# Attention maxima turned by VectorE in 32x32 blocks and placed by eight transfers, instead of one TensorE transpose, one ScalarE copy and two transfers

## The chip, the cores and the metric

The kernel runs on one core of one Trainium2 chip. The metric is the device time of one execution in microseconds (us); three runs of the kernel before gave a median of 2221.6 us (2217.65 to 2241.77 us).

## The reference

One transformer block on `x` of 8 sequences, 1024 tokens each, 256 features, all float32. First attention with 16 heads of 16 features, then a mixture of 8 experts. What matters here is the attention, where keys and values are the same projection:

```python
q = x @ Wq
kv = x @ Wkv
q, kv = rotary(split(q)), rotary(split(kv))     # (8 * 16 heads, 1024, 16)
q = q * SCALE
att = jnp.einsum('bmd,bnd->bmn', q, kv)
attn = jax.nn.softmax(att, axis=-1)
out = jnp.einsum('bij,bjd->bid', attn, kv)
```

The softmax subtracts each row's maximum before the exponential.

## The kernel before, in words

The program has four parts, one after the other with small overlaps: projection (`project`), attention (`attend`), what finishes the attention and chooses tokens, and the experts. The change touches only `attend`.

**Pairs and groups.** Attention works on 64 pairs of heads (8 sequences, 8 pairs each). A pair takes 16 groups (`NG = 16`). In each group TensorE does, in `body` of `tensor`: two score products of the pair (`scores`, L681, into the ring `a_st` of three PSUM slots), two products for the row maxima of a later pair (`maxima`, L718, into the two slots of `a_sm`), and eight small products of probabilities and values (`values`, L705, into `a_pv`). ScalarE takes each score slot and writes its exponential to `a_prob` (`exp`, L844): 32 a pair. VectorE reduces each `a_sm` slot to negated maxima (`reduce`, L770): 16 a pair.

**The maxima of a pair are found one pair ahead.** In the second half of pair q's own groups and the first half of the next, maxima of the pair after are reduced: while pair q is scored, groups 0 to 7 finish the maxima of pair q+1 and groups 8 to 15 begin those of pair q+2. After group 7 VectorE combines the two halves (`a_nm`, L778). GpSimd cuts the result into a high and a low part (`split`, L809 and L811, into `a_nsplit`).

**From columns to rows.** The scores are taken transposed (keys on partitions, queries along the free dimension), so the maxima must be subtracted along the free dimension. The kernel does this inside the score product: the negated maxima stand as two extra rows (high and low part) of the query tile `a_q`, against rows of ones in `a_k`. The maxima come out of the reduction as columns, one per partition, and so must be turned into rows. Before the change this takes five steps, for pair q+1 during pair q: TensorE transposes `a_nsplit` into a slot of the score ring ahead of group 12 (`turn_maxima`, L689); ScalarE copies 32 rows of 128 from there to `a_mrow` (`copy_max_rows`, L858) and so frees the slot; SyncE issues two transfers `a_q<-a_mrow`, one per head (`max_rows`, L543); and TensorE's first score product of pair q+1 waits for them:

```python
if u == 0:
    pe.wait_ge(m_in, (q.n + 1) * 32)
```

**SyncE's queue.** SyncE (SP) issues all transfers of attention in one order per pair q (`body` of `sync`): nine loads for pair q+2 (`load`, L528 and L534), which wait until pair q-1 has all its scores; the reciprocals of pair q-2 (`put_rden`, L614); the raw output of pair q-1 (`store`, L642); the scaled output of pair q-3 (`put_on`, L624); `fetch_rden` of pair q-2 (L618); the maxima rows of pair q+1 (`max_rows`, L543); and two fetches of pair q-1 (`fetch`, L607 and L609). Each waits for what it needs, and everything behind it waits with it.

**GpSimd's order** per pair q is `split(q)`, `place(q+2)`, `scale(q-3)`:

```python
split(q)
if not q.first() and q.plus(2).exists():
    place(q.plus(2))
if q.follows(3):
    scale(pool, q.plus(-3))
```

`place` (L819) copies the values just loaded, the last of the nine loads, and waits for them to land. `scale` (L572) makes the result that `put_on` stores. So `put_on` for pair q-3 comes after the landing of the values of pair q+2, because GpSimd does the one behind the other.

**The start.** The rows of pair 0 are turned while TensorE makes maxima of pair 1. ScalarE itself issues their two transfers, while SyncE is still busy with the last stores of the projection.

## Time and profile before

| | us |
|---|---|
| median of three runs | 2221.6 |
| lowest and highest run | 2217.65, 2241.77 |
| the profiled execution's own time | 2217.65 |
| its span, first to last instruction | 2217.7 |
| attention, first score product to last exponential | 273.8 to 1586.2 |

The profile is of one execution, the 2217.65 us one; its span is its time. PE is TensorE's matrix products, PEld its weight loads, DVE is VectorE, ACT ScalarE, POOL GpSimd, SP SyncE; a q behind an engine's name means its instruction queue (SPq issues transfers). A row of the chronological view gives start, length, engine, line, operation, output and inputs, count, and in brackets how long the engine was idle before and what ended that.

### The profile page before, as it was taken

To read this page: it belongs to the slowest core of one execution; us is meant where nothing else is said; L and a number is where in the kernel's file an instruction comes from. 1 tells how busy PE (TensorE), PEld (TensorE's weight loads), DVE (VectorE), ACT (ScalarE), POOL (GpSimd) and SP (SyncE) were. 2 spreads that over 40 slices of the span, in tenths; PEclk is the share of its full clock that TensorE was granted. 3 is DMA by queue.
4 is the path that set the end of the run, shared out by engine and by line. 5 is a ranking of instruction groups with operands and counts; after the bars stand their busy time and mean duration, and the time that the engine had idled before them with its cause. 6 is when DMAs were issued, how large, how long until landed. Compare 5 with 4: busy or idle time off the path is not lost. (4 is left out here: it accounts for less than half of the span.)

```text
span 2217.7 us, 53241 instructions
## 1 busy us (share of the span) xinstructions
PE 2004.8 (90%) x16684; PEld 1046.9 (47%) x16684; DVE 1950.9 (88%) x3221; ACT 1503.4 (68%) x2842; POOL 648.3 (29%) x864
## 2 busy tenths in 40 slices
PE   6777699999999999999999999999988129999998
PEld 3344233333333333333333333333577128999997
DVE  7888889999999999999999999999489679888863
ACT  3444278888888888888888888888645014554443
POOL 7788300110111011011111101111277015565653
PEclk9999689999999999999999999999999559999999
DMA  2666644344344444434433443444476023443432
GB/s 88 219 222 214 183 116 77 71 82 86 71 78 83 77 73 83 83 72 80 83 76 74 82 85 70 80 83 90 143 257 205 30 79 82 101 93 85 103 66 29
DMA packets 152543, 224.62 MB, mean 101 GB/s; under 512 B 34855, under 2 KB 104970, under 8 KB 152458
## 3 DMA queue, kind: packets, MB, share of 16 engines
q1 hardware_dynamic: 131814, 197.89, 38.2%
q0 software_dynamic: 12288, 17.05, 4.5%
q10 hardware_dynamic: 8356, 8.67, 1.1%
q8 instruction: 39, 0.64, 0.1%
q14 instruction: 46, 0.38, 0.1%
HBM read 129.38 MB, written 93.06 MB: 100 GB/s over the span
## 5 line engine op out<-in xcount | busy, mean ns | idle before, releaser
L770 DVE TENSOR_REDUCE a_mx<-a_sm 128x2 f32<-128x1024 f32 x1024 | 1234.8, 1223 | 56.1 <-PE a_sm L718 42.8
L844 ACT ACTIVATE a_prob<-a_st 128x512 f32<-128x512 f32 x2048 | 1113.1, 597 | 170.7 <-PE a_st L681 139.7
L681 PE MATMUL a_st<-a_q,a_k 50*128 50x512 f32 x2048 | 752.9, 448 | 5.7 <-DMA a_q<-a_mrow 5.7
L718 PE MATMUL a_sm<-a_k,a_q 48*128 48x512 f32 x2048 | 748.0, 455 | 9.7 <-DVE a_mx L770 8.0
L705 PE MATMUL a_pv<-a_prob,a_v 128*32 128x256 f32 x8192 | 657.1, 393 | 23.1 <-ACT a_oraw L851 22.5
L681 PEld LDWEIGHTS a_st<-a_q,a_k 50*128 50x128 f32 x2048 | 312.3, 186 | 412.0 <-ACT a_prob L844 391.8
L819 POOL TENSOR_TENSOR a_v<-a_v_raw,a_zero 128x256 f32<-128x256 f32 x64 | 39.6, 620 | 1065.2 <-DMA a_v_raw<-values 1065.2
L705 PEld LDWEIGHTS a_pv<-a_prob,a_v 128*32 128x32 f32 x8192 | 161.9, 108 | 395.7 <-issue 192.2
L718 PEld LDWEIGHTS a_sm<-a_k,a_q 48*128 48x128 f32 x2048 | 304.7, 188 | 22.7 <-DVE a_mx L770 20.6
L1771 ACT ACTIVATE e_hT<-e_ps_h,e_b1b 128x512 f32<-128x512 f32 x128 | 88.3, 690 | 204.3 <-PE e_ps_h L1808 192.3
L1808 PE MATMUL e_ps_o<-e_w_high,e_hT_high 128*128 128x256 f32 x512 | 145.9, 285 | 0.0
L1808 PE MATMUL e_ps_o<-e_w_high,e_hT_low 128*128 128x256 f32 x512 | 144.8, 283 | 0.0
L1808 PE MATMUL e_ps_o<-e_w_low,e_hT_high 128*128 128x256 f32 x512 | 144.8, 283 | 0.0
L1661 DVE TENSOR_TENSOR e_hT_low<-e_hT,e_hT_high 128x512 fp32r<-128x512 f32 x128 | 86.5, 690 | 47.4 <-ACT e_hT_high L1777 36.6
L381 PE MATMUL p_ps_q<-p_w,p_xnT 128*128 128x512 f32 x256 | 128.0, 625 | 0.0
L1724 POOL TENSOR_TENSOR e_ahead<-l_row_no 128x1 f32<-128x1 f32 x72 | 49.1, 682 | 245.4 <-DVE e_idx L1617 158.3
L1747 POOL DMA_INDIRECT out_dram<-e_ob,e_idx x64 | 112.0, 1750 | 13.9 <-issue 8.7
L345 ACT COPY p_qkv<-p_ps_q 128x512 f32<-128x512 f32 x64 | 37.5, 585 | 94.8 <-PE p_ps_q L381 55.0
L1808 PE MATMUL e_ps_h<-e_yT_high,e_w_high 128*128 128x512 f32 x256 | 101.4, 396 | 0.0
L1808 PE MATMUL e_ps_h<-e_yT_low,e_w_high 128*128 128x512 f32 x256 | 100.4, 392 | 0.0
L1808 PE MATMUL e_ps_h<-e_yT_high,e_w_low 128*128 128x512 f32 x256 | 100.3, 392 | 0.0
L307 POOL TENSOR_TENSOR p_tsin<-p_qkv,p_sin 128x256 f32<-128x256 f32 x128 | 98.1, 786 | 3.7 <-ACT p_qkv L345 3.7
(146 smaller groups left out, 2368.2 us busy)
## 6 DMA issues: line engine op xcount, KB each, us to landing
qkv_parts<-p_parts SPq DMA_DIRECT2D x64, 512.0 KB
a_q<-qkv_parts SPq DMA_DIRECT2D x128, 128.0 KB, 3.5
a_k<-qkv_parts SPq DMA_DIRECT2D x128, 128.0 KB, 4.4
attended<-a_oraw SPq DMA_DIRECT2D x64, 256.0 KB, 4.2
e_w<-in_fc_dram SPq DMA_DIRECT2D x16, 1024.0 KB, 5.4
token_table<-f_tab ACTq DMA_DIRECT2D x8, 1056.0 KB, 4.7
p_x<-in_x_dram SPq DMA_DIRECT2D x16, 512.0 KB, 8.0
values<-p_values SPq DMA_DIRECT2D x8, 1024.0 KB, 20.0
```

Source lines behind the costliest of these rows:

```text
L307: nc.gpsimd.tensor_tensor(ts[:, :, h * HALF:(h + 1) * HALF], src[:, :, (1 - h) * HALF:(2 - h) * HALF], sinb[:, i:i + 1, h * HALF:(h + 1) * ...
L381: mm = nc.tensor.matmul(ps_q[:, k % 2], xnT[:, k % 2, c], w[:, c], start=(c == 0), stop=(c == DC - 1))
L681: nc.tensor.matmul(st[:, slot % RING], kb[rows, q.buf, jt * P:(jt + 1) * P], qb[rows, q.buf, ic * CHUNK:(ic + 1) * CHUNK], start=True, sto ...
L705: mm = nc.tensor.matmul(pv[row:row + 2 * DH, cols], vb[:, q.buf, jt, h, :], prob[:, jt % 2, h, start:start + QUARTER], start=(jt == 0 and ...
L718: mm = nc.tensor.matmul(sm[:, slot, h], qb[rows, q.buf, qt * P:(qt + 1) * P], kb[rows, q.buf, kc * CHUNK:(kc + 1) * CHUNK], start=True, st ...
L770: nc.vector.tensor_reduce(mx[:, qt, kc, :], sm[:, slot], AX.X, ALU.max, negate=True).then_inc(max_done, 1)
L844: nc.scalar.activation(prob[:, jt % 2, h, ic * CHUNK:(ic + 1) * CHUNK], st[:, slot % RING], ACT.Exp, scale=DH ** -0.5).then_inc(drained, 1)
L1661: nc.vector.tensor_tensor(group_of(hT_low, g), hT[:, g % 4], group_of(hT_high, g), ALU.subtract).then_inc(hT_low_done, 1)
L1724: nc.gpsimd.tensor_tensor(ahead[:], row_no[:], row_no[:], ALU.add).then_inc(ahead_done, 1)
L1747: nc.gpsimd.indirect_dma_start(out=out_rows, out_offset=bass.IndirectOffsetOnAxis(ap=idx[:, k, i:i + 1], axis=0), in_=ob[:, i], in_offset= ...
L1771: nc.scalar.activation(hT[:, g % 4], ps_h[:, g % 3], ACT.Gelu_apprx_tanh, bias=b1b[:, k, g % FC:g % FC + 1]).then_inc(gelu_done, 1)
L1808: return nc.tensor.matmul(to, weights, moving, start=first, stop=last)
```

## The change

VectorE transposes `a_nsplit` (now 128x32 in place of 128x128, of which 32 columns held data before) straight into `a_mrow` (now 128x32) in one instruction. The instruction turns each 32x32 block by itself: block b of 32 tokens lands in partitions 32b to 32b+31, as rows of 32 elements. It comes after ten groups of the pair (`TURN_AT = 10`; TensorE's transpose stood ahead of group 12). TensorE's transpose, ScalarE's copy and the extra slot of the score ring go, and so does the identity matrix that attention loaded. As the 1024 maxima of a head now lie in four blocks of partitions, each head takes four transfers of 16 rows x 32 elements in place of one of 16 x 128: eight per pair in place of two. VectorE waits for `n2_done` (GpSimd's cut) and for the eight transfers of the pair before; GpSimd's cut waits for the transpose before (`turned`).

```diff
-    TURN_AT = 12
-    TURN_FILL = 2 * TURN_AT
-    FILLS = 2 * NG + 1
+    TURN_AT = 10
+    FILLS = 2 * NG
+    BLOCK = 32
+    BLOCKS = P // BLOCK
+    MAX_ROWS = CUTS * TILES
...
-    nsplit = a.sb("a_nsplit", [P, P], F32R)
+    nsplit = a.sb("a_nsplit", [P, BLOCK], F32R)
-    mrow = a.sb("a_mrow", [2 * CUTS * TILES, P])
+    mrow = a.sb("a_mrow", [P, BLOCK])
...
     def fill_of(q, u):
-        turns = 1 if u >= TURN_FILL and q.plus(1).exists() else 0
-        return 1 + u + turns, q.n * FILLS + (1 + u + turns)
+        return (q.c * FILLS + u) % RING, q.n * FILLS + u
...
-    def max_rows(eng, q, turned):
-
-        eng.wait_ge(drained, turned + 1)
-        rows = CUTS * TILES
+    def max_rows(eng, q):
+
+        eng.wait_ge(turned, q.n + 1)
         for h in range(2):
             top = HEAD_ROWS * h + DATA_ROWS
-            eng.dma_start(qb[top:top + CUTS, q.buf, :].bitcast(F32).rearrange("r (t c) -> r t c", c=P),
-                          mrow[h * rows:(h + 1) * rows, :]).then_inc(m_in, 16)
+            to = qb[top:top + CUTS, q.buf, :].bitcast(F32).rearrange("r (t b c) -> r t b c", b=BLOCKS, c=BLOCK)
+            for b in range(BLOCKS):
+                row = b * BLOCK + h * MAX_ROWS
+                eng.dma_start(to[:, :, b, :], mrow[row:row + MAX_ROWS, :]).then_inc(m_in, 16)
...
             if u == 0:
-                pe.wait_ge(m_in, (q.n + 1) * 32)
+                pe.wait_ge(m_in, (q.n + 1) * 32 * BLOCKS)
...
-        def turn_maxima(q, slot, n):
-            pe.wait_ge(n2_done, q.n + 1)
-            if not q.first():
-                pe.wait_ge(drained, n - (RING - 1))
-            nc.tensor.transpose(st[:, slot % RING, 0:P], nsplit[:].bitcast(F32), ident[:]).then_inc(filled, 1)
...
+        def turn_maxima(q):
+
+            dve.wait_ge(n2_done, q.n + 1)
+            if not q.first():
+
+                dve.wait_ge(m_in, q.n * 32 * BLOCKS)
+            nc.vector.transpose(mrow[:], nsplit[:].bitcast(F32)).then_inc(turned, 1)
...
+                if g == TURN_AT and q.plus(1).exists():
+                    turn_maxima(q.plus(1))
...
         for v in range(NG // 2):
             reduce(Pair(0, 1, 1), v, NG + v, v % 2)
+            if v == 1:
+                turn_maxima(Pair(0, 0, 0))
...
-                pool.wait_ge(filled, 1 + (q.n - 1) * FILLS)
+                pool.wait_ge(turned, q.n)
...
-        def copy_max_rows(q, slot, n):
-            act.wait_ge(filled, n + 1)
-            if not q.first():
-
-                act.wait_ge(m_in, q.n * 32)
-            nc.scalar.copy(mrow[:], st[0:2 * CUTS * TILES, slot % RING, 0:P]).then_inc(drained, 1)
...
-        copy_max_rows(Pair(0, 0, 0), 0, 0)
-        max_rows(act, Pair(0, 0, 0), 0)
+        max_rows(act, Pair(0, 0, 0))
```

Where it moves instructions, in the order of the program (REGISTER_ALU, ISA and the like are the queue's own bookkeeping):

SyncE's queue within the loop over pairs, from the scaled output to the next pair's loads; first the kernel before.

```order
L624 DMA attended_normalised<-a_on 2x16x512
L617 REGISTER_ALU
L618 DMA a_rrep<-reciprocal_denominators 64x1x512
L539 REGISTER_ALU
L543 DMA a_q<-a_mrow 2x8x128 x2
L602 REGISTER_ALU
L607 ISA
L607 DMA a_den<-attended 128x1x16
L609 DMA a_num<-attended 64x1x512
L523 ISA
L528 ISA
L528 DMA a_q<-qkv_parts 32x1024
```

The changed kernel in the same place.

```order
L620 DMA attended_normalised<-a_on 2x16x512
L613 REGISTER_ALU
L614 DMA a_rrep<-reciprocal_denominators 64x1x512
L541 DMA a_q<-a_mrow 2x8x32 x8
L598 REGISTER_ALU
L603 ISA
L603 DMA a_den<-attended 128x1x16
L605 DMA a_num<-attended 64x1x512
L519 ISA
L524 ISA
L524 DMA a_q<-qkv_parts 32x1024
```

The two transfers of the maxima are now eight, in the same place of the queue, ahead of the two fetches and the next loads.

VectorE within the loop over pairs, from the combining of the two halves on, in the kernel before.

```order
L778 TENSOR_TENSOR a_nm<-a_mx 128x16
L769 REGISTER_ALU
L770 TENSOR_REDUCE a_mx<-a_sm 128x2
L769 REGISTER_ALU
L770 TENSOR_REDUCE a_mx<-a_sm 128x2
L769 REGISTER_ALU
L770 TENSOR_REDUCE a_mx<-a_sm 128x2
```

The changed kernel in the same place.

```order
L763 TENSOR_TENSOR a_nm<-a_mx 128x16
L754 REGISTER_ALU
L755 TENSOR_REDUCE a_mx<-a_sm 128x2
L754 REGISTER_ALU
L755 TENSOR_REDUCE a_mx<-a_sm 128x2
L770 ISA
L771 STREAM_TRANSPOSE a_mrow<-a_nsplit 128x32
L754 REGISTER_ALU
L755 TENSOR_REDUCE a_mx<-a_sm 128x2
```

The transpose stands behind the second reduction after the combining of the halves.

## Rows read from the trace of the kernel before

**Rows 1.** The page, parts 1 and 2: engine, busy us, share; then by slices.

```profile
PE 2004.8 (90%) x16684; PEld 1046.9 (47%) x16684; DVE 1950.9 (88%) x3221; ACT 1503.4 (68%) x2842; POOL 648.3 (29%) x864
...
PEclk9999689999999999999999999999999559999999
```

**Rows 2.** Windows: at the start and in mid-attention, busy us of each engine, clock, DMA.

```profile
255.00:275.00 20.00, 10.67 (x31) 4.23 (x29) 14.45 (x14) 0.62 (x2) 0.46 (x2) 0.50 0.52 166
...
400.00:1500.00 1100.00, 1080.31 (x10381) 405.42 (x10377) 1060.09 (x969) 968.35 (x1828) 124.73 (x216) 1.00 0.43 79
```

**Rows 3.** Chronology around 909 us: PE at the transpose, and group 0 of the next pair.

```profile
909.42 0.33 PE L689 MATMUL a_st<-a_ident,a_nsplit 128*128 128x128 f32 x1
909.68 0.50 PE L681 MATMUL a_st<-a_q,a_k 50*128 50x512 f32 x1
...
914.63 0.50 PE L681 MATMUL a_st<-a_q,a_k 50*128 50x512 f32 x1
```

**Rows 4.** The same chronology, VectorE.

```profile
905.34 0.18 DVE L778 TENSOR_TENSOR a_nm<-a_mx 128x16 f32<-128x16 f32 x1
905.64 4.62 DVE L770 TENSOR_REDUCE a_mx<-a_sm 128x2 f32<-128x1024 f32 x4
910.49 8.66 DVE L770 TENSOR_REDUCE a_mx<-a_sm 128x2 f32<-128x1024 f32 x7 [0.23 <-PE a_sm L718]
919.06 0.24 DVE L563 RECIPROCAL a_rden<-a_den 128x16 f32<-128x16 f32 x1
```

**Rows 5.** SyncE's waits from 400 to 1500 us: total, times, longest.

```profile
SPq L624 <- POOL a_on L572: 281.5, 54, 6.4
SPq L543 <- ACT a_mrow L858: 122.1, 53, 3.4
SPq L528 <- PE a_st L681: 40.0, 54, 0.9
```

**Rows 6.** The tile `a_mrow` from 400 to 1500 us: duration ns, first and last start.

```profile
L543 SPq DMA_DIRECT2D a_q<-a_mrow x106: 627/642/662, 418.4 to 1483.1; - x106
L858 ACT COPY a_mrow<-a_st x53: 254/256/256, 418.1 to 1482.1; 32x128 f32<-32x128 f32 x53
```

**Rows 7.** Chronology of SyncE's queue over one pair.

```profile
893.94 0.82 SPq L528 DMA_DIRECT2D a_q<-qkv_parts  x2
...
897.93 0.36 SPq L534 DMA_DIRECT2D a_v_raw<-values  x1
...
905.62 1.63 SPq L624 DMA_DIRECT2D attended_normalised<-a_on  x2
907.35 0.63 SPq L618 DMA_DIRECT2D a_rrep<-reciprocal_denominators  x1
910.14 1.34 SPq L543 DMA_DIRECT2D a_q<-a_mrow  x2
```

**Rows 8.** Chronology of GpSimd in the same pair.

```profile
903.61 0.62 POOL L819 TENSOR_TENSOR a_v<-a_v_raw,a_zero 128x256 f32<-128x256 f32 x1 [17.79 <-DMA a_v_raw<-values]
904.19 1.27 POOL L572 TENSOR_TENSOR a_on<-a_num,a_rrep 64x512 f32<-64x512 f32 x1
...
905.99 0.23 POOL L811 TENSOR_TENSOR a_nsplit<-a_nm,a_nsplit 128x16 fp32r<-128x16 f32 x1
```

**Rows 9.** Transfers in two windows: 912.07 to 912.50, and 912.50 to 913.1 us.

```profile
DMA packets 27, 0.01 MB, mean 29 GB/s; under 512 B 3, under 2 KB 27, under 8 KB 27
...
DMA packets 0, 0.00 MB, mean 0 GB/s; under 512 B 0, under 2 KB 0, under 8 KB 0
```

**Rows 10.** Chronology of the start of attention: ScalarE, SyncE's queue, TensorE.

```profile
261.58 0.25 ACT L858 COPY a_mrow<-a_st 32x128 f32<-32x128 f32 x1 [21.15 <-PE a_st L689]
261.87 4.19 ACTq L543 DMA_DIRECT2D a_q<-a_mrow  x2
...
247.57 27.30 SPq L178 DMA_DIRECT2D qkv_parts<-p_parts  x8
...
273.84 0.76 PE L681 MATMUL a_st<-a_q,a_k 50*128 50x512 f32 x1 [5.74 <-DMA a_q<-a_mrow]
```

More of the change, by code:

```diff
@@ L412, with attend @@
 K_RUNS = ((0, 0, 1), (DH, 0, 2))
-def attend(nc, ctx, own, parts_dram, v_dram, o_dram, rden_dram, on_dram, ident_d):
+def attend(nc, ctx, own, parts_dram, v_dram, o_dram, rden_dram, on_dram):
     NG = 2 * TILES
-    TURN_AT = 12
-    TURN_FILL = 2 * TURN_AT
-    FILLS = 2 * NG + 1
+    TURN_AT = 10
[3 more added lines that the diff above has]
+    MAX_ROWS = CUTS * TILES
     AHEAD = NG + NG // 2
@@ L426, in attend @@
     a = Alloc(nc, ctx)
-    ident = a.sb("a_ident", [P, P])
     qb = a.sb("a_q", [P, 3, N], F32R)
@@ L450, in attend @@
     set_up = a.sem("a_set_up")
-    ident_in = a.sem("a_ident_in")
     ones_in = a.sem("a_ones_in")
@@ L469, in attend @@
     n2_done = a.sem("a_n2_done")
+    turned = a.sem("a_turned")
     filled = a.sem("a_filled")
@@ L508, in fill_of @@
     def fill_of(q, u):
-        turns = 1 if u >= TURN_FILL and q.plus(1).exists() else 0
-        return 1 + u + turns, q.n * FILLS + (1 + u + turns)
-    def turn_of(q):
-        return 1 + TURN_FILL, q.n * FILLS + (1 + TURN_FILL)
+        return (q.c * FILLS + u) % RING, q.n * FILLS + u
     def head_rows(h, rows):
@@ L521, in load @@
         if not (q.p is not None and q.p < 3):
-            sp.wait_ge(filled, 1 + (q.n - 2) * FILLS)
+            sp.wait_ge(filled, (q.n - 2) * FILLS)
         for h in range(2):
@@ L593, in banks_left @@
         pe.wait_ge(max_done, NP * NG)
-        pe.wait_ge(drained, 1 + NP * FILLS - 1)
+        pe.wait_ge(drained, NP * FILLS)
         pe.wait_ge(evac_done, NP)
@@ L657, in body @@
             if q.plus(1).exists():
-                max_rows(sp, q.plus(1), turn_of(q)[1])
+                max_rows(sp, q.plus(1))
             if not q.first():
@@ L675, in scores @@
             if u == 0:
-                pe.wait_ge(m_in, (q.n + 1) * 32)
-            if not (q.first() and slot < RING):
+                pe.wait_ge(m_in, (q.n + 1) * 32 * BLOCKS)
+            if not (q.first() and u < RING):
                 pe.wait_ge(drained, n - (RING - 1))
@@ L727, in body @@
                 v = (g + NG // 2) % NG
-                if g == TURN_AT and q.plus(1).exists():
-                    turn_maxima(q.plus(1), *turn_of(q))
                 scores(q, 2 * g)
@@ L753, in tensor @@
                 maxima(q1, v, v % 2, h)
-            if v == 1:
-                pe.wait_ge(ident_in, 16)
-                turn_maxima(q0, 0, 0)
         pe.wait_ge(ones_in, 32)
@@ L796, in set_buffers @@
         nc.gpsimd.memset(vb[:], 1.0).then_inc(set_up, 1)
-        nc.gpsimd.memset(nsplit[:].bitcast(F32), 0.0).then_inc(set_up, 1)
         nc.gpsimd.memset(ones[:], 1.0).then_inc(set_up, 1)
@@ L801, in split @@
         def split(q):
-            part = [nsplit[:, 0:2 * CUTS * TILES].rearrange("p (h s t) -> p s t h", h=2, s=CUTS)[:, s]
+            part = [nsplit[:].rearrange("p (h s t) -> p s t h", h=2, s=CUTS)[:, s]
                     for s in range(CUTS)]
@@ L828, in body @@
                 scale(pool, q.plus(-3))
-        pool.wait_ge(set_up, 4)
+        pool.wait_ge(set_up, 3)
         for p in range(3):
@@ L863, in body @@
                     evacuate(q.plus(-1))
-                if u == TURN_FILL and q.plus(1).exists():
-                    copy_max_rows(q.plus(1), *turn_of(q))
                 exp(q, u)
-        copy_max_rows(Pair(0, 0, 0), 0, 0)
-        max_rows(act, Pair(0, 0, 0), 0)
+        max_rows(act, Pair(0, 0, 0))
         pairs(act, body)
@@ L1865, in project_attend_finish @@
              settle_second, settle_last) = attend(nc, ctx, own, parts, values.rearrange("b r p n -> (b r) p n"), o, rden,
-                                                  on, t["ident"])
+                                                  on)
         early = Early(nc, ctx)
```

3 lines of the change are left out of this document (1 added, 2 removed).

## Prediction

> **What bounds the kernel now.** I read the page first: TensorE is busy 90% of the span and VectorE 88%, and the clock digits stand at full through attention except at its start [rows 1]. Windows then show mid-attention alone: of 1100 us TensorE is busy 1080, VectorE 1060, ScalarE 968, GpSimd 125, at full clock [rows 2]. The tile view of `a_mrow` gives the pace: 53 copies, the first at 418.1 and the last at 1482.1 us, so 52 pairs take 1064 us, 20.46 us each [rows 6]. The chronology shows how a pair passes: TensorE reaches its transpose at 909.42, goes on with group 12 at 909.68, and begins group 0 of the next pair at 914.63 with no wait in front of it [rows 3]. So TensorE sets the pace, VectorE follows closely behind, and the transfers that bring the maxima rows are in time.
>
> How much in time is the question here, because the change puts six more transfers into SyncE's queue. The queue's waits from 400 to 1500 us answer it: it waits 5.2 us a pair for GpSimd's scaled output (281.5 in 54), 2.30 us for the copied maxima (122.1 in 53), and 0.74 us for the scores in front of the next loads (40.0 in 54) [rows 5]. Only the last two are spare time. The first isn't, as the chronologies show: the loads are issued from 893.94, the values last of them at 897.93 [rows 7]; GpSimd's `place` starts at 903.61 when they have landed, `scale` runs from 904.19 to 905.46 [rows 8], and only then can SyncE issue the scaled output, then `fetch_rden` (done at 907.98), then the maxima rows. A later load moves all of this. So SyncE's queue is a ring that closes on itself: loads, landing, `place`, `scale`, scaled output, maxima rows, fetches, loads. Its length without the spare time is 20.46 - 2.30 - 0.74 = 17.42 us. It has 3.04 us left in a pair.
>
> **The change, part by part.**
>
> *TensorE's transpose goes.* It holds the stream from 909.42 to 909.68 [rows 3]: 0.26 us a pair, 63 times, 16 us at most, if TensorE stays the bound.
>
> *ScalarE's copy goes*, 0.256 us a pair [rows 6]. ScalarE is busy 968 of 1100 us [rows 2] and the copy's room is the same gap that the transpose makes. I price it at nothing beside the 0.26 us: it costs nothing to leave it out, and the most that it could bring is its own length, 63 times, 16 us more.
>
> *VectorE's transpose comes.* The trace has no such instruction. From below the nearest is the combining of 128x16, 0.18 us; from above the reciprocal of 128x16, 0.24 us, and with the restart of the reductions behind it 0.30 us (905.34 to 905.64) [rows 4]. I take 0.3 us with its restart. Is it hidden? After the combining VectorE has a backlog and works it off: four reductions in 4.62 us, so one every 1.13 us ((4.62 - 1.22) / 3, one alone being 1.22) against TensorE's group of about 1.23 [rows 4]. The transpose falls in this backlog; the third of the four would start 0.3 us late, and TensorE, which may run two groups ahead in the ring `a_sm`, might wait some tenths. Alone that gives back 0 to 0.3 of the 0.26 us saved: the computing engines end between equal and 16 us faster. Below, a longer wait covers it altogether. Its own wait for `n2_done` is met: GpSimd's cut ends at 906.22 [rows 8], and the tenth group's reduction ends at about 905.64 + 1.13 + 1.22 = 908.0 [rows 4].
>
> *Two transfers become eight.* One takes 0.642 us of SyncE's queue [rows 6], the second of two ends 1.34 us after the start of the first [rows 7], so each further one adds 0.70 us, and six add 4.2 us. They are smaller in data, with as many pieces (16 rows). Two kinds of transfer stand in the queue: the loads of many whole rows, 0.36 to 0.41 us each, and those that go to few outer rows, from 0.63 us over the old maxima rows to the scaled output's 0.82 (1.63 for two) [rows 7]. So the bounds for one more are 0.40 and 0.82 us, and I take 0.70, the old rows' own step, as the new ones write the same two partitions as the old.
>
> Behind these rows stands a rule of the Trainium skill (DMA: Bandwidth & Descriptors, "Why a DMA increments its semaphore by 16 and not by 1"): the number of DMA engines that a transfer uses divides the slowest dimension of both sides, and the issuing sequencer itself writes the remaining counts. The maxima rows have a slowest dimension of 2 before and after, a load 16 or 32; by this rule the new transfers stay in the dear class, and the sum stays; were each placed like a load, six would add 2.4 us and the ring would just not bind.
>
> 4.2 us is more than the 3.04 us of spare time. The ring becomes 17.42 + 4.2 = 21.62 us, 1.16 us longer than the pair of now. It holds where a pair issues loads for the pair two ahead and maxima rows for the next: pairs 1 to 61, 61 times, 71 us. For the last pairs, without loads, the turning of the maxima sets the time, about 1 us once more. TensorE then stands still over 1 us at each pair's first score product, and what it saved by the transpose is lost in this wait, and VectorE's addition too. Behind SyncE's eight transfers wait the two fetches and nine loads; by the ring they are what hurts, not the rows' own landing. TensorE's clock I leave at full: a wait of 1.2 in 21.6 us is short beside the 5.74 us at the start.
>
> *The start.* Pair 0's rows are issued by ScalarE: two transfers took 4.19 us, 2.1 each, with SyncE's eight stores of 27.30 us beside them, and TensorE stood until 273.84, of which the view counts 5.74 us as a wait for these rows [rows 10]. Six more at 2.1 us are 12.6 us. VectorE's transpose comes after two more reductions, about 1 us later than the old copy's end. Together some 13 us, once. Bounds: six at 0.64 us give 4 us, six at the stores' 3.41 us (27.30 / 8) give 20 us. The stretch before this is at half clock [rows 2], and pair 0 is shifted with it, not stretched.
>
> Identity load, wider memset and ring slot: nothing on the path; they cost and bring less than 0.5 us, since the start is bound by the maxima rows.
>
> **Sum:** 2217.65 (the execution profiled, against a median of 2221.6) + 71 + 1 + 13 = 2303 us. By the median it would be 4 us more, which the range holds.
>
> **The rivals.**
>
> *A, my forecast: SyncE's ring binds,* 2303 us, own range 2275 to 2335: the values' landing varies, and 0.4 us more or less per pair is 24 us.
>
> *B: the turning binds, not the ring.* If the loads land faster when nothing else of the queue is beside them, the ring gets shorter than the way from group 0 to the next: VectorE's transpose ends about 908.3, which is 14.1 us after group 0 (914.63 [rows 3] less a pair of 20.46 is 894.17); eight transfers take 7 x 0.70 + 0.64 = 5.5 us; landing takes 1.0 us (the old transfers' issue ends at 911.48; the last packets come before 912.50, none after [rows 9]). That is 20.6 to 20.8 us a pair, 0.2 us over the present 20.46, 12 to 20 us in all, with the start 2248 us. For it: landing is the largest and least certain piece of the ring. Against it: the traffic is the same as now, so there is no reason for loads to land nearly 1 us sooner.
>
> Here the Trainium skill has another figure (same page, "Anatomy of one DMA"): a fixed cost of about 2.0 us per transfer, most of it the receipt of the write. With it B would have 1 us more a pair and end near A; the trace's 1.0 us speaks against it for a transfer within SBUF.
>
> *C: more transfers cost next to nothing in the queue (no slower than before).* The price is one transfer's issue, the place SyncE's queue, and the point of decision 3.04 / 6 = 0.51 us: below it the ring stays under 20.46 us. At 0.40 us the eighth ends 14.1 + 3.2 = 17.3 us after group 0, and TensorE doesn't wait. Then 0 to 16 us are saved, say 8, against 4 us at the start: about 2213 us. For it: loads at 0.40 us in the same queue, and smaller transfers. Against: each of 106 old ones took 0.627 us or more [rows 6].
>
> The same page's "Anatomy of one DMA" leans to C: setup is small, and many descriptors may be issued before their cost shows. By it C's 2213 us would come out; the rows show the queue held for each transfer's 0.64 us, so I give it little.
>
> *D: the transfers get dearer in a row.* Eight behind each other on few DMA engines could hold the queue as ScalarE's did at the start (2.1 us under load). At 0.9 us each the ring is 17.42 - 1.34 + 7.2 = 23.3 us, 2.8 us over, 171 us in all, with the start near 2400 us.
>
> **How the numbers follow.** A 0.65, B 0.14, C 0.13, D 0.06, anything else 0.02. The predicted time is A's, 2303 us. The range from 2248 to 2345 us takes in B, A and the half of D that is nearest; C and the rest of D are left out, 0.18. A measurement of this kernel can tell about 1%, 22 us, from no change. Faster by over 1% needs more than the 16 us that TensorE's transpose is worth: 0.03. Within 1%: the rest of C and the low end of B, 0.11. Slower: 0.86.
>
> **What would show it.** In the changed profile: pairs at about 21.6 us by the first and last of VectorE's transposes; SyncE's eight transfers at 0.64 us each, ending 5.5 us after their start; SyncE no longer waiting at the maxima rows nor in front of the loads, but still about 5 us for the scaled output; a new wait of TensorE for the transfers `a_q<-a_mrow` of about 1.2 us in most pairs; VectorE's transpose 0.18 to 0.3 us long; the first score product near 287 us. A wait of SyncE for the transpose with TensorE still waiting means B. No wait of TensorE and pairs of 20.2 to 20.5 us mean C, and the forecast would be wrong at the price of a transfer. Pairs above 22.2 us mean D or a slower landing.

## The result, and the profile after

| | before | after |
|---|---|---|
| median of the runs, us | 2220.57 (4 runs) | 2300.87 (4 runs: 2284.22, 2295.61, 2306.13, 2325.98) |
| profiled execution, us (its span) | 2217.65 (2217.7) | 2284.22 (2282.4) |
| ratio, with its 95% interval | 1 | 1.0333 [1.0289, 1.0376] |

Ratios, here and below, leave out single disturbed runs (here the one of 2325.98; later one of 6731.58 among the ten of the kernel with `scale` first, and one of the kernel before), so this one is a little smaller than the quotient of the medians. The change makes the kernel slower by 3.3%. The forecast was 2303 us, from 2248 to 2345.

The page of the kernel after, parts 1 and 2: engine, busy us, share of the span, instructions; then the granted clock by slices. It answers to [rows 1].

```profile
PE 2031.2 (89%) x16620; PEld 1047.5 (46%) x16620; DVE 1982.6 (87%) x3285; ACT 1491.4 (65%) x2778; POOL 650.4 (28%) x863
...
PEclk9999599999999999999899999999999559999999
```

TensorE does fewer instructions than before and is busy 26 us longer. The second line points to a reason: one digit in mid-attention is an 8, so the clock wasn't at full throughout, as it was before. The windows show it (columns as in [rows 2]: length, busy of TensorE, weight loads, VectorE, ScalarE and GpSimd, granted clock, DMA share, GB/s).

```profile
400.00:1500.00 1100.00, 1057.97 (x9782) 390.62 (x9782) 1031.07 (x969) 909.06 (x1682) 116.62 (x202) 0.98 0.37 74
1072.00:1092.00 20.00, 18.28 (x180) 6.76 (x176) 17.91 (x19) 16.08 (x31) 2.27 (x4) 1.00 0.39 68
1092.80:1113.30 20.50, 20.50 (x118) 6.53 (x116) 12.52 (x14) 11.41 (x21) 2.30 (x4) 0.50 0.37 75
```

In the same 1100 us TensorE gets through 9782 matmuls where it did 10381. Two things are in that. In the second window it stands still for 1.7 of 20 us, at full clock: a wait in each pair. In the third it never stands still and does 118 matmuls in 20.5 us: its clock is at 0.50, the lower of its two levels (1.2 GHz).

The pair in numbers, taken at each pair's first score product of group 0 (L681 before, L677 after), median over the pairs at full clock, in us; the times within a pair count from that product. (By the mean the pair is 20.46 us before and 21.29 us after.)

| | first transfer of the rows starts | last one ends | first load issued | last load of queries or keys landed | next pair |
|---|---|---|---|---|---|
| before | 15.91 | 17.26 | -0.29 | 8.65 | 20.4 |
| after | 14.92 | 20.16 | 0.86 | 9.97 | 21.3 |

The eight transfers end 2.9 us later than the two did, though they start 1.0 us sooner; the loads are issued 1.15 us later.

SyncE's waits from 400 to 1500 us in the kernel after (total, times, longest), against [rows 5]:

```profile
SPq L620 <- POOL a_on L568: 291.8, 50, 6.6
SPq L541 <- DVE a_mrow L771: 11.0, 5, 5.7
SPq L610 <- DVE a_rden L559: 5.1, 5, 1.8
SPq L524 <- PE a_st L677: 0.3, 1, 0.3
```

The 2.30 us a pair in front of the maxima rows and the 0.74 us in front of the loads are gone: 11.0 us (in 5 pairs) and 0.3 us remain of 122.1 and 40.0. What stays is the wait for GpSimd's scaled output. SyncE's queue has no spare time left; it is the ring that the prediction describes.

The queue's chronology over the same stretch of a pair as [rows 7]:

```profile
963.45 0.82 SPq L524 DMA_DIRECT2D a_q<-qkv_parts  x2
...
967.38 0.36 SPq L530 DMA_DIRECT2D a_v_raw<-values  x1
...
974.87 1.64 SPq L620 DMA_DIRECT2D attended_normalised<-a_on  x2
976.71 0.63 SPq L614 DMA_DIRECT2D a_rrep<-reciprocal_denominators  x1
977.39 5.26 SPq L541 DMA_DIRECT2D a_q<-a_mrow  x8
983.00 0.63 SPq L603 DMA_DIRECT2D a_den<-attended  x1
983.73 0.61 SPq L605 DMA_DIRECT2D a_num<-attended  x1
```

The eight transfers hold the queue for 5.26 us where two held it for 1.34: 3.92 us for six, 0.653 us each. From the values' issue (967.38) the chain goes on in GpSimd:

```profile
972.86 0.62 POOL L815 TENSOR_TENSOR a_v<-a_v_raw,a_zero 128x256 f32<-128x256 f32 x1 [18.70 <-DMA a_v_raw<-values]
973.44 1.28 POOL L568 TENSOR_TENSOR a_on<-a_num,a_rrep 64x512 f32<-64x512 f32 x1
```

`place` starts 5.5 us after the values' issue, when they have landed; `scale` follows, `scale` ends at 974.72, and SyncE issues the scaled output at 974.87. Nothing in this chain waits for anything but its predecessor. VectorE in the same stretch:

```profile
973.81 0.94 DVE L763 TENSOR_TENSOR a_nm<-a_mx 128x16 f32<-128x16 f32 x1
974.87 2.36 DVE L755 TENSOR_REDUCE a_mx<-a_sm 128x2 f32<-128x1024 f32 x2
977.14 0.20 DVE L771 STREAM_TRANSPOSE a_mrow<-a_nsplit 128x32 f32<-128x32 f32 x1
```

Here is something that the prediction didn't have. The combining of the maxima took 0.18 us in the pair shown before [rows 4] and takes 0.94 us here. It starts while GpSimd's `scale` runs and ends at 974.75, with it (974.72). The tile views of `a_nm` say that this has become the rule (min/median/max in ns); the kernel after:

```profile
L763 DVE TENSOR_TENSOR a_nm<-a_mx x64: 175/848/1302, 260.2 to 1626.8; 128x16 f32<-128x16 f32 x64
```

and the kernel before:

```profile
L778 DVE TENSOR_TENSOR a_nm<-a_mx x64: 174/176/1044, 260.2 to 1559.4; 128x16 f32<-128x16 f32 x64
```

Over 0.2 us are 51 of the 64 after and 16 of the 64 before: the meeting was there already, in one pair of four, and the late loads, which push `scale` back, have made it usual. The Trainium skill has the rule (SBUF — State Buffer, "SBUF: two separate sides"): VectorE and GpSimd share a pair of ports, held for a whole instruction; a VectorE instruction with two SBUF inputs and a GpSimd one that reads SBUF shut each other out. The trace agrees: the combining has two such inputs, and in all 47 pairs of the kernel after in which it starts while `scale` runs it ends 31 to 36 ns behind it.

So the transpose (977.14, 0.20 us) ends at 977.34, just as SyncE is through with its fetch; the transfers begin at 977.39. By this pair one can't say which of the two holds them, and that was what the experiments had to tell apart.

Waits of VectorE (first line) and TensorE from 400 to 1500 us in the kernel after:

```profile
DVE a_mx L755 <- PE a_sm L708: 56.2, 120, 1.8
PEld a_sm L708 <- DVE a_mx L755: 20.6, 39, 0.9
PE a_st L677 <- DMA a_q<-a_mrow: 12.9, 27, 1.4
```

The forecast wait at the first score product is there, but only in 27 pairs and 0.48 us in the mean. Group by group, TensorE's time within a pair is longer in three places, by the means: group 0 by 0.10 us, group 10 by 0.53 us (it takes 1.81 us) and group 15 by 0.37 us; group 11 is 0.25 us shorter, where the transpose stood. At group 10 stands the stretched combining: VectorE falls behind, and TensorE waits for a free half of `a_sm`. The sum is what the ring asks for in the mean; where in the pair TensorE waits is decided by who is late first.

The tile view of `a_mrow` gives the transfer and the transpose (ns), against [rows 6]:

```profile
L541 SPq DMA_DIRECT2D a_q<-a_mrow x408: 596/611/662, 401.6 to 1486.5; - x136
L771 DVE STREAM_TRANSPOSE a_mrow<-a_nsplit x51: 199/201/203, 401.3 to 1481.7; 128x32 f32<-128x32 f32 x51
```

From the first to the last transpose are 50 pairs in 1080.4 us, 21.61 us each. That looks like the forecast 21.62, but is a mean over two things: pairs at full clock take 21.3 us, and the four with a stretch of half clock in them 21.6, 23.0, 24.5 and 28.7.

**The account** of the two profiled executions. The first score product of pair 1 comes 4.4 us later (300.4 to 304.8). From there to pair 62 it takes 1310.9 us where it took 1248.0: 62.9 us, of which 61 x (21.29 - 20.46) = 51 are the longer pairs and the other 12 the half clock. (There are 41 us at half clock; they cost less than their half, since not all of TensorE's time in a pair goes by its clock: at half of it 118 matmuls pass in 20.5 us, against 180 in 20.) From pair 62 to the end of the span it is 2.6 us shorter. That is 64.7 us of span; 1.8 lie outside it.

### The profile page after: what moved, and what is told of

Read it like the earlier page. It is cut to its first block and busy times, and to the rows that moved or that the text cites. A ratio compares the mean times of both kernels' runs of the same rounds, so it can differ in the third digit from the quotient of the medians.

```text
span 2282.4 us, 53254 instructions
## 1 busy us (share of the span) xinstructions
PE 2031.2 (89%) x16620; PEld 1047.5 (46%) x16620; DVE 1982.6 (87%) x3285; ACT 1491.4 (65%) x2778; POOL 650.4 (28%) x863
## 5 line engine op out<-in xcount | busy, mean ns | idle before, releaser
L677 PE MATMUL a_st<-a_q,a_k 50*128 50x512 f32 x2048 | 775.9, 453 | 31.0 <-DMA a_q<-a_mrow 27.5
L708 PE MATMUL a_sm<-a_k,a_q 48*128 48x512 f32 x2048 | 747.0, 463 | 20.6 <-DVE a_mx L755 18.2
L695 PE MATMUL a_pv<-a_prob,a_v 128*32 128x256 f32 x8192 | 664.3, 396 | 21.9 <-ACT a_oraw L847 21.3
L677 PEld LDWEIGHTS a_st<-a_q,a_k 50*128 50x128 f32 x2048 | 317.5, 187 | 465.8 <-ACT a_prob L840 424.2
```

What stands on the lines that cost most here:

```text
L677: nc.tensor.matmul(st[:, slot % RING], kb[rows, q.buf, jt * P:(jt + 1) * P], qb[rows, q.buf, ic * CHUNK:(ic + 1) * CHUNK], start=True, sto ...
L695: mm = nc.tensor.matmul(pv[row:row + 2 * DH, cols], vb[:, q.buf, jt, h, :], prob[:, jt % 2, h, start:start + QUARTER], start=(jt == 0 and ...
L708: mm = nc.tensor.matmul(sm[:, slot, h], qb[rows, q.buf, qt * P:(qt + 1) * P], kb[rows, q.buf, kc * CHUNK:(kc + 1) * CHUNK], start=True, st ...
```

## The experiments

The rivals after the result: the ring through SyncE's queue (A), the turning way with its eight transfers and their landing (B), whether the time comes from the number of transfers at all or from the transpose on VectorE, and the clock. "Pair" is the mean over the pairs at full clock; where the median lies apart from it, both are given. The edits are shown without what only follows from them (the counts of the waits, and zeros or ones that fill what is no longer written).

### Two transfers with the new transpose

```diff
-            for b in range(BLOCKS):
-                row = b * BLOCK + h * MAX_ROWS
-                eng.dma_start(to[:, :, b, :], mrow[row:row + MAX_ROWS, :]).then_inc(m_in, 16)
+            eng.dma_start(qb[top:top + CUTS, q.buf, :].bitcast(F32).rearrange("r (t c) -> r t c", c=P),
+                          mrow[h * MAX_ROWS:(h + 1) * MAX_ROWS, :]).then_inc(m_in, 16)
```

> The changed kernel, but with two transfers of 16 rows x 128 a pair in place of eight of 16 x 32. Only the first 32 columns of a_mrow hold turned maxima, the others hold zeros, so three quarters of the maxima are left out; every instruction but the six transfers stays. Ring theory (SyncE's queue of loads, landing, place, scale, output and maxima rows closes on itself and is too long with eight): the ring is 17.4 us, so TensorE binds again, pairs of 20.2 to 20.5 us, time 2200 to 2220 us, no wait of TensorE for the rows. Turning theory (from group 0 to the end of VectorE's transpose, then eight transfers in a row, is too long): the same, since two transfers take 1.3 us. Rival that blames VectorE's transpose itself, or its combining of maxima held up by GpSimd: pairs stay above 20.9 us, time above 2245 us.

Measured: 2208.19 us, ratio 0.9912 [0.9878, 0.9945]; pair 20.26 us; no half clock. SyncE's waits in it, from 400 to 1500 us:

```profile
SPq L538 <- DVE a_mrow L771: 154.0, 54, 3.2
SPq L618 <- POOL a_on L566: 148.5, 54, 3.5
SPq L524 <- PE a_st L675: 137.9, 54, 2.7
```

It follows that VectorE's transpose does no harm, and that TensorE's was worth about 0.20 us a pair (20.46 to 20.26) of the 0.26 us that it held the stream. Without the six further transfers the loss is gone.

The queue waits 2.85 us for the maxima and 2.55 us in front of the loads in every pair, so the ring is wide open. That is 5.4 us of spare time where a ring of 17.42 us would leave 2.84. The other 2.6 us come from the loads: the DMA views from 400 to 1500 us (size, median us from issue to landing) have, in this kernel and in the kernel before,

```profile
a_v_raw<-values SPq DMA_DIRECT2D x55, 128.0 KB, 2.8
```

```profile
a_v_raw<-values SPq DMA_DIRECT2D x54, 128.0 KB, 5.3
```

In all other kernels here the values take 4.9 to 5.5 us. Why they land sooner in this one no run shows. So this kernel differs by more than its six transfers, and for the length of the ring the kernel with six transfers, below, is the cleaner one.

### Eight transfers, turned by TensorE as before

The kernel before, with the copied rows carried in pieces of 32 columns.

```diff
-            eng.dma_start(qb[top:top + CUTS, q.buf, :].bitcast(F32).rearrange("r (t c) -> r t c", c=P),
-                          mrow[h * rows:(h + 1) * rows, :]).then_inc(m_in, 16)
+            to = qb[top:top + CUTS, q.buf, :].bitcast(F32).rearrange("r (t b c) -> r t b c", b=4, c=32)
+            for b in range(4):
+                eng.dma_start(to[:, :, b, :], mrow[h * rows:(h + 1) * rows, b * 32:(b + 1) * 32]).then_inc(m_in, 16)
```

> The kernel before, with TensorE's transpose and ScalarE's copy, but the rows placed by eight transfers of 16 rows x 32. At the 0.653 us step of the changed kernel's transfers six more are 3.9 us. Ring theory: pairs of 17.4 + 3.9 = 21.3 us, time about 2217.65 + 54 + 8 for the start = 2280 us. Turning theory: the copy ends 15.9 us after group 0, eight transfers take 5.2 us and landing 1.2 us, so pairs of 22.3 us and about 2340 us. Rival that blames VectorE: no slower than before, 2220 us.

Measured: 2661.11 us, ratio 1.1888 [1.1806, 1.1969]; pair 22.8 us, median 22.6, from the dozen pairs that are at full clock throughout. This is far above what either theory gave, and the window of the attention (columns as above) shows why:

```profile
300.00:1560.00 1260.00, 1173.58 (x8945) 413.90 (x8943) 923.05 (x833) 841.67 (x1576) 103.40 (x182) 0.78 0.28 58
```

The mean granted clock is 0.78. The waits of TensorE and of SyncE's queue from 400 to 1500 us in the same kernel:

```profile
PE a_st L682 <- DMA a_q<-a_mrow: 65.7, 35, 1.9
```

```profile
SPq L545 <- ACT a_mrow L859: 241.0, 40, 12.2
```

In 35 pairs TensorE waits 1.9 us for the rows, and SyncE waits for ScalarE's copy: here it is the turning way that binds (B), since TensorE's transpose comes so late. The copy ends 16.15 us after group 0 here (15.9 in the kernel before); with 5.25 us of transfers and 1.17 of landing that is 22.6, the measured median. But the larger part of the loss is another: behind these waits the clock fell, in 43 stretches of 758 us together. The longer pairs alone would give 2228 + 62 x (22.6 - 20.46) = 2360 us; the other 300 are the clock. Neither theory had a term for this.

### Two transfers and six idle ones

The kernel before, with six small transfers of constants that nobody reads, issued behind the rows.

```diff
             eng.dma_start(qb[top:top + CUTS, q.buf, :].bitcast(F32).rearrange("r (t c) -> r t c", c=P),
                           mrow[h * rows:(h + 1) * rows, :]).then_inc(m_in, 16)
+        for i in range(6):
+            eng.dma_start(num[ROWS + 2 * i:ROWS + 2 * i + CUTS, 0, 0:TILES * 32].rearrange("r (t c) -> r t c", c=32),
+                          ident[i % 2 * rows:(i % 2 + 1) * rows, 0:32]).then_inc(idle_in, 16)
```

> The kernel before with its two transfers of maxima rows, and behind them in SyncE's queue six more of 16 rows x 32 that carry nothing needed (constants into unused partitions) and that TensorE doesn't wait for; ScalarE's copy of the next pair waits for them, which is a pair later. Ring theory: pairs of 21.3 us as if the transfers were needed, about 2275 us. Turning theory: TensorE's rows leave as before, so pairs of 20.46 us and 2218 to 2225 us.

Measured: 2531.9 us in the middle of four runs (2470.26 to 2562.18); pair 21.6 to 21.9 us, near what the ring gives, but with 631 us at half clock in 23 stretches. So the time is missed by a wide margin. Its waits of TensorE from 400 to 1500 us hold one that the kernels above don't have:

```profile
PE a_sm L723 <- DMA a_k<-qkv_parts: 31.9, 26, 2.0
```

The loads come so late (2.84 us after group 0, where they came 0.29 us before it) that the keys of the pair two ahead land at 11.7 us, when TensorE's products for the maxima already need them: group 8 takes 2.39 us. That pushes TensorE's transpose and ScalarE's copy back, and with them the start of the rows' transfers, from 15.9 to 17.5 us, and the next loads. It is a second ring, which closes over the transpose, the transfers and the loads. The length of a pair comes out about right, for a reason that I had not expected, so this kernel is no clean test of A.

### The changed kernel with the transpose one group earlier

```diff
-    TURN_AT = 10
+    TURN_AT = 9
```

> The changed kernel with VectorE's transpose one reduction earlier (TURN_AT 9 in place of 10), 1.13 us earlier in the pair. Ring theory: SyncE comes to the maxima rows no earlier, so pairs stay at 21.3 us and the time within 10 us of the changed kernel (2284 to 2306). Turning theory: the rows leave 1.1 us earlier, pairs of about 20.2 to 20.3 us, time near 2230 us.

Measured: 2271.83 us, ratio 1.0189 [1.0159, 1.022]; pair 21.3 us, the eight transfers from 14.96 to 20.21 us after group 0, as in the kernel after (14.92 to 20.16). The maxima are turned 1.1 us sooner and the rows don't leave any sooner (the time is just below the range expected, the pair is as expected); SyncE's only wait from 400 to 1500 us is

```profile
SPq L620 <- POOL a_on L568: 308.6, 52, 6.4
```

That decides between A and B: it isn't the turning way. It also decides about the stretched combining, which is as common here as in the kernel after: of the pairs 2 to 60, 45 have one over 0.25 us and 14 don't, and they are 21.31 and 21.29 us long in the mean. And it bears on a third thing. The pairs are as long as in the kernel after, yet by the ratios the kernel is 1.4% faster (1.0189 against 1.0333, intervals apart). The kernel after has 41 us at half clock in its profiled execution, this one none:

```profile
300.00:1560.00 1260.00, 1212.99 (x11360) 449.83 (x11352) 1191.35 (x1123) 1055.42 (x1952) 133.66 (x234) 1.00 0.37 75
```

TensorE's longest idle time among the pairs is 0.9 us in it, against 1.45 us in the kernel after.

### Scaled output ahead of the values

If the ring closes over the landing of the values only because GpSimd does `place` before `scale`, then exchanging the two opens it without touching a transfer. `scale` needs nothing of the values.

```diff
-            if not q.first() and q.plus(2).exists():
-                place(q.plus(2))
...
+            if not q.first() and q.plus(2).exists():
+                place(q.plus(2))
```

(It now stands behind the call of `scale`.)

> The changed kernel with GpSimd's scale(q-3) ahead of its place(q+2): the scaled output no longer stands behind the landing of the loads, so SyncE's queue is no longer a ring through the loads; all eight transfers stay. Ring theory: what is left is the turning way, 14.2 us to the end of VectorE's transpose, 5.25 us for eight transfers, 1.17 us to the first score product, so pairs of 20.6 us, time 2218 to 2240 us, and SyncE's wait for the scaled output (5.8 us a pair in the changed kernel) gone. Rival, eight small transfers are slow by themselves wherever they stand, or VectorE's combining held up by GpSimd is the cost: pairs stay at 21.3 us, time 2270 us or more.

Measured: 2229.94 us, ratio 1.0035 [1.0016, 1.0055]; pair 20.48 us; no half clock among the pairs; eight transfers as before. SyncE's waits:

```profile
SPq L541 <- DVE a_mrow L771: 154.8, 54, 3.5
SPq L614 <- DMA reciprocal_denominators<-a_rden: 119.0, 54, 2.7
```

The wait for the scaled output is gone, and 2.9 us a pair in front of the rows are back. With it go 71 us by the medians, 66 by the ratios; the pairs are worth 49 us (61 x (21.29 - 20.48)), and most of the rest is half clock, of which the kernel after has 12 us in its fastest run and more in the others. That shows the ring by opening it.

The edit takes away two things at once, the ring and the meeting of `scale` with the combining. The meeting has a price of its own where the ring is open: in the kernel before, of the pairs 2 to 60, the 13 with a combining over 0.25 us take 20.63 us in the mean and the other 46 take 20.41; the longest, 1.04 us, lies in a pair of 21.22. Where the ring binds it has none, as the 14 and the 45 pairs above show. So the ring is the cause of the 21.3, and with the ring opened by some other edit the meeting could still cost some tenths.

Now the turning way sets the pair: the transfers end 19.32 us after group 0, landing takes 1.17 us, together 20.49. That is B's length, which the prediction had put at 20.6 to 20.8. The combining of the maxima is back at a median of 0.18 us, as `scale` no longer meets it.

The same with `TURN_AT = 9`:

> As the one before, and VectorE's transpose one reduction earlier. With the ring open the turning now counts: the rows are in place 1.1 us earlier than TensorE asks for them less 0.3, so pairs of 20.26 us as with two transfers, time 2203 to 2217 us (8 to 11 us over the kernel with two transfers, for the start). Rival, the order of GpSimd has nothing to do with it: 2270 us as with the earlier turning alone.

Measured: 2210.9 us, ratio 0.9954 [0.993, 0.9979]; pair 20.15 us, the last transfer ending at 18.04. Now the transfers are in time, the saved slot of TensorE comes out, and the kernel comes out 0.5% below the kernel before.

### Six transfers in the changed kernel

```diff
-            for b in range(BLOCKS):
+            for b in range(BLOCKS - 1):
```

> The changed kernel with six of the eight transfers: the maxima of one block of 32 tokens in four are left out (ones stand in their place), the order of GpSimd is as in the changed kernel. Ring theory: 17.42 + 4 x 0.653 = 20.0 us, just under the 20.26 us of TensorE's own stream, so pairs of 20.3 to 20.6 us and a time of 2205 to 2225 us. Rival, each transfer costs its share wherever it stands (six extra cost 1.05 us a pair, so four 0.70 us): pairs of 20.96 us, about 2255 us.

Measured: 2213.04 us, ratio 0.997 [0.995, 0.9991]; pair 20.23 us.

```profile
SPq L623 <- POOL a_on L571: 294.5, 54, 6.1
SPq L613 <- DVE a_rden L562: 28.5, 54, 0.7
SPq L541 <- DVE a_mrow L774: 8.7, 25, 0.7
```

With four more than two, the ring is 17.42 + 4 x 0.653 = 20.03 us long, just below TensorE's own 20.23, and small waits in front of the rows are back in the queue. (The values land after 5.4 us here, as in the kernel before.) With six more it is 21.34. The pair goes 20.26, 20.23, 21.3 for two, six and eight transfers. So there is no price per transfer, only a length of queue from which it costs.

### The new order of GpSimd in three other kernels

The kernel before with `scale` ahead of `place` (the same edit):

> The kernel before with only GpSimd's order changed, scale(q-3) ahead of place(q+2). Ring theory: before the change the ring has 3 us left and doesn't bind, so no difference, 2215 to 2228 us, pairs of 20.46 us. Rival, the gain of the scale-first kernels comes from GpSimd's order itself: faster than before by 10 us or more.

Measured in 8 runs: 2213.21 us, ratio 0.9946 [0.9917, 0.9974], 2 us below the range expected; pair 20.40 us against a mean of 20.46 (median 20.40). The 0.06 us are the pairs with a stretched combining, which there are none of here; 61 times that is 4 us and not the 12 measured, so the half per cent was doubtful, and was measured again (below).

The kernel with six idle transfers and this order:

> The kernel before with the six idle transfers a pair, and scale(q-3) ahead of place(q+2). Ring theory: the ring is open, the idle transfers have room, pairs of 20.5 us, no half clock after the start, time 2218 to 2235 us against 2532 us with the ring closed. Rival, six more transfers load the DMA engines or the queue so that they cost wherever they stand: 2275 us or more.

Measured: 2522.09 us, ratio 1.1369 [1.1289, 1.1449]; pair 21.7 to 22.05. A miss, and a useful one: the order of GpSimd changes nothing here, so the ring of this kernel doesn't go over `scale`. TensorE waits for the keys here too (26 times from 400 to 1500 us, 1.4 us in the mean, 35.6 us together), as in the ring told above.

The kernel with eight transfers turned by TensorE, and this order:

> The kernel before with its maxima rows placed by eight transfers, and scale(q-3) ahead of place(q+2). Here the turning way alone is too long, whatever the ring: TensorE's transpose ahead of group 12 and ScalarE's copy end 15.9 us after group 0, and 5.25 + 1.17 us follow, so at full clock pairs of 22.3 us, TensorE idle 1.9 us at each pair's first product, and the clock falling to half as often as before: 2600 to 2680 us. Rival, the ring was the cause here too: back to 2220 to 2240 us.

Measured: 2685.38 us, ratio 1.206 [1.2017, 1.2102]; pair 22.48; 826 us at half clock. The time is a little above the range expected, and nothing is gained: the turning way over TensorE doesn't pass `scale` either.

### Again, with twelve runs each

The kernel before with `scale` first:

> The kernel before with scale(q-3) ahead of place(q+2), again, on one chip with the next. 2208 to 2218 us, 0.3 to 0.6% below the kernel before: the first time it came out 0.5% faster, of which the trace of one execution shows 0.06 us a pair and an earlier first score product.

Measured: 2229.23 us, ratio 1.0002 [0.9979, 1.0025]; pair 20.51 us. The half per cent of the eight runs isn't there, and the expectation missed: the order alone brings nothing to the kernel before that these runs can show. The same kernel's pair is 20.40 us on one chip and 20.51 us on another, so tenths of a microsecond, and half a per cent, compare safely only within one chip.

The changed kernel with `scale` first and the transpose one group earlier:

> The changed kernel with scale first and the transpose one reduction earlier, beside the one above. Pairs of 20.15 us against 20.40 us save 15 us, the start (eight transfers issued by ScalarE under load, and a longer half clock) costs about 13 us: within 5 us of the one above. Rival, the start costs less in most executions: 10 us or more below it.

Measured: 2213.17 us, ratio 0.9939 [0.992, 0.9958]; pair 20.27 us, against 20.51 in the kernel above on the same chip. The expectation, within 5 us of the kernel above, missed and its rival held: the time is 16 us below, of which the pairs give 61 x 0.24 = 15. The first score products of pairs 0 and 1 stand at 279.0 and 303.4 us, 5 and 3 us later than before. Twice measured, it is 0.5% and 0.6% below the kernel before.

## Why the prediction was right, and where only by luck

**The ring (A): right.** The three waits of the queue were read rightly: 3.04 us were spare, the 5.2 us in front of the scaled output were not. Opening the ring by an edit on another engine takes 71 us away; turning sooner takes nothing away from the pair; six transfers fit, eight don't. What the sum takes as fixed, the landing of the loads, held in every kernel but the one with two transfers.

**The size of a transfer: a little too dear.** The prediction added 0.70 us for each further one, from one pair of transfers. In a row of eight each further one added 0.653 us (3.92 / 6; from start to start within the row it is 0.653 us too, by the median). With this the ring is 17.42 + 3.92 = 21.34 us, and 21.3 were measured. The term of 71 us should have been 54, and measured 51. The prediction put the new transfers in the class of the old ones, by the number of outer rows, beside a rule of the Trainium skill (DMA: Bandwidth & Descriptors, "Why a DMA increments its semaphore by 16 and not by 1"). The class came out, 0.611 us against the old 0.642 and the loads' 0.36 to 0.41. That the outer rows are the reason isn't shown: the two fetches fill 128 and 64 partitions and take 0.63 and 0.61 us.

The other section of the same page that it drew on ("Anatomy of one DMA — SWDGE (gpsimd) path") describes transfers issued through GpSimd's path, which the prediction doesn't say. For SyncE's queue the trace decides: with three quarters less data in a transfer it is held for 0.61 instead of 0.64 us, each time, so the cost of one more shows at once.

**The start: the transfers too dear, the whole open.** Forecast were 13 us. ScalarE's eight transfers and the first score product of the kernel after:

```profile
262.91 11.11 ACTq L541 DMA_DIRECT2D a_q<-a_mrow  x8
...
281.93 0.76 PE L677 MATMUL a_st<-a_q,a_k 50*128 50x512 f32 x1 [13.71 <-DMA a_q<-a_mrow]
```

Each takes 1.39 us and not 2.1; group 0 comes 8.1 us later than before and not 13, and by pair 1 only 4.4 us are left of it. Pair 0 was not just shifted: it took 26.5 us before and 22.9 us here. But this is one execution, the fastest of its four. In the profiled executions of the other kernels that start in the same way (turned earlier, `scale` first, and both, twice) the first product of pair 1 stands at 309.8, 312.6, 314.5 and 303.4 us, 3 to 14 us later than before. It stands late where the half clock of the start lasts long, to 304.7, 311.2 and 318.6 us in the first three; it ends at 292.0 us in the last, at 290.7 in the kernel after and at 291.3 in the kernel before. So the 13 us aren't refuted for every execution. The size of the term goes with the length of the half clock, which the forecast had only shifted; what sets that length stays open.

**The last pairs** were forecast 1 us longer; from pair 62 on the kernel is 2.6 us shorter. TensorE has no transpose and no wait there.

**"TensorE's clock I leave at full": wrong, and the step that failed.** The reason given was that a wait of 1.2 in 21.6 us is short beside the 5.74 us at the start. This is the step at which 41 us of half clock came in, a cost of 12 us in the profiled execution and, by their mean clocks, more in the other three. TensorE around 1090 us in the kernel after, at group 0:

```profile
1090.89 0.49 PE L677 MATMUL a_st<-a_q,a_k 50*128 50x512 f32 x1 [1.36 <-DMA a_q<-a_mrow]
...
1091.66 0.64 PE L695 MATMUL a_pv<-a_prob,a_v 128*32 128x256 f32 x8
...
1092.90 1.08 PE L695 MATMUL a_pv<-a_prob,a_v 128*32 128x256 f32 x8
```

An idle time of 1.36 us, and 2 us later the same eight matmuls take 1.08 us instead of 0.64; it lasts 20 us, a whole pair. It happened four times among the pairs, each time 0.4 to 2 us after the end of an idle time of 1.24 to 1.45 us, out of seven such times over 1.2 us. Over the four executions the time rises as the mean clock falls: 2284 us at 0.950, 2296 at 0.945, 2306 at 0.940, 2326 at 0.929. Without any of it among the pairs (in the profiled execution), at the same length of pair, the kernel with the earlier turning takes 2272.

So the forecast of 2303 us against 2300.87 flatters. By its own terms, rightly sized, it would have been 2217.65 + 51 + 4 - 3 = 2270 us with this execution's start, and 2278 with the start of the kernel with `scale` first; terms that were too large (the pairs by 20 us, the last pairs by 4, the start by up to 9) stood in for the one that was missing. The mechanism was right, and that the number lies within 2 us of the median is luck.

**The new wait: in the wrong place.** The prediction had TensorE stand about 1.2 us at the first score product in most pairs. It stands there 0.48 us in 27 pairs, and about half of the loss sits at group 10, where the combining meets `scale`. The prediction took the combining at 0.18 us as fixed, and that was the oversight: the tile view of the kernel before already had one of 1.04 us, and the prediction itself moved `scale` to a later time and didn't ask what runs on VectorE then. It made no difference in the sum, because the ring set the pair: with the transpose moved ahead of it (`TURN_AT = 9`) the pair stayed at 21.3.

**VectorE's transpose:** 0.201 us, inside the bounds of 0.18 and 0.3. TensorE's transpose gave back 0.20 of 0.26 us where the ring is open (0.24 by the two kernels on one chip), and nothing where it isn't, as said.

**The rivals.** B: the way isn't the bound in the changed kernel, but with the ring open it is, at 20.49 us. C falls: a further transfer costs the queue 0.653 us, above the point of 0.51. D falls: 0.653 in a row and not 0.9.

## What to carry to other kernels

Before adding transfers to a queue, look whether it closes on itself through another engine, and count only those waits of it as spare that don't move with the loads; the price of one more is nothing up to that sum and its full issue time, in every pair, from there on. Where such a ring binds, look at the order on the engine that it passes: one instruction that waits for a landing stood ahead of one that didn't need it, and exchanging the two was worth 71 us, nearly the whole damage. And waits of one to two microseconds in a stream of matmuls can cost a multiple of their own length once more in clock: here 5.4 us of waits cost 12 us, 55 waits of 1.88 us some 300, and the 24 waits over 1 us in the kernel with six idle transfers, 32 us together, some 250 (1572.4 us from pair 1 to 62, less 61 x 21.66). So give them a term of their own.

## What the runs showed of the hardware that I had not expected

*The clock can fall behind single short idle times.* The idle times on TensorE among the pairs and the time at half clock, each from one profiled execution:

| kernel | longest idle time, us | idle times over 1 us | half clock from pair 1 to 61, us |
|---|---|---|---|
| before | under 0.5 | 0 | 0 |
| after | 1.45 | 7 | 41 |
| after, turned one group earlier | 0.9 | 0 | 0 |
| before, six idle transfers | 1.96 | 24 | 631 |
| before, eight transfers | 1.99 | 55 | 758 |

TensorE was busy 91% of the 20 us ahead of the fall at 1092.8 (18.28 us, the second window of the result). The Trainium skill (TensorE: Matmul & The Clock Gate, "Why this matters for your kernels") warns of idle gaps between bursts of matmuls; those that it speaks of are longer than any here, and the measurement decides. Why three of the seven in the kernel after brought no fall stays open; no run here was made to settle it. The length of the idle time alone doesn't decide: in the two kernels with six idle transfers falls also came behind 0.91 and 0.88 us, while the kernel turned earlier has idle times up to 0.88 us and no fall.

*What one of these transfers costs the queue depends little on its size.* In SyncE's queue a transfer of 2x8x32 elements takes 0.611 us (596 to 662 ns), one of 2x8x128 takes 0.642 us: a quarter of the data saves 5%. On ScalarE's queue at the start, with SyncE's stores beside them, the same small ones take 1.39 us each; whether the queue or the stores make the difference no run here tells apart.

*Landing within SBUF* took 1.17 us from the end of the last transfer's issue (977.39 + 5.26 = 982.65) to the matmul that waited for it:

```profile
983.82 0.49 PE L677 MATMUL a_st<-a_q,a_k 50*128 50x512 f32 x1 [0.24 <-DMA a_q<-a_mrow]
```
